# A GRU inside a four-layer kernel: input products in blocks of 24 steps in place of 32

## What is computed

```python
def cell(h, x):
    gi = x @ W_ih + b_ih            # [B, 3 D]: does not depend on h
    gh = h @ W_hh + b_hh            # [B, 3 D]: needs the state before
    i_r, i_z, i_n = jnp.split(gi, 3, axis=-1)
    h_r, h_z, h_n = jnp.split(gh, 3, axis=-1)
    r = jax.nn.sigmoid(i_r + h_r)
    z = jax.nn.sigmoid(i_z + h_z)
    n = jnp.tanh(i_n + r * h_n)
    h_new = (1.0 - z) * n + z * h
    return (h_new, h_new)

_, hs = jax.lax.scan(cell, initial_state, xs)   # 256 steps; B = 8, D = 512
x = x + hs
```

## Time and profile before

| | |
|---|---|
| median of 3 runs | 2070.93 us (2069.5 to 2075.49) |
| the profiled execution | 2068.51 us |
| its span, first to last instruction | 2066.7 us |
| TensorE, busy share of the span | 90% |
| VectorE, ScalarE, GpSimd | 61%, 53%, 18% |
| mean granted clock of TensorE | 0.873 |

### The profile page before, as it was taken

How to read it: one execution, slowest core, us unless ns; L and a number is a source line. 1 busy time by engine, 2 the same in 40 slices (tenths; PEclk the granted TensorE clock), 3 DMA queues, 4 the chain that set the end, 5 groups by cost and what they waited for, 6 DMA issues and landing times. The chain is left out here.

```text
span 2066.7 us, 86137 instructions
## 1 busy us (share of the span) xinstructions
PE 1857.9 (90%) x32542; PEld 1377.3 (67%) x32542; DVE 1257.9 (61%) x5543; ACT 1097.8 (53%) x4105; POOL 377.3 (18%) x1398
## 2 busy tenths in 40 slices
PE   8877998999989989899888899999998999999876
PEld 4234454463644646455556898989898989999875
DVE  5545383654835447363343677777777777777766
ACT  0342736636355363645644565656565655656554
POOL 3000000000000000000000334343434333333335
PEclk7788999999999999999999796969797988879556
DMA  5222213222032220413223000000000000000002
GB/s 175 77 78 53 79 29 94 66 55 87 20 105 56 71 89 1 117 28 73 72 62 108 1 1 0 0 0 0 0 0 0 0 0 0 0 0 0 0 0 82
DMA packets 103527, 86.76 MB, mean 42 GB/s; under 512 B 15616, under 2 KB 90496, under 8 KB 103440
## 3 DMA queue, kind: packets, MB, share of 16 engines
q1 hardware_dynamic: 101392, 84.38, 14.2%
q10 hardware_dynamic: 1664, 1.18, 0.2%
q0 software_dynamic: 384, 0.01, 0.0%
HBM read 60.20 MB, written 21.00 MB: 39 GB/s over the span
## 5 line engine op out<-in xcount | busy, mean ns | idle before, releaser
L1255 PE MATMUL bank_pair_A<-moving,rep 128*128 128x16 f16 x8192 | 327.7, 172 | 55.3 <-DVE moving L1494 49.5
L1255 PEld LDWEIGHTS bank_pair_A<-moving,rep 128*128 128x128 f16 x8192 | 277.8, 99 | 75.6 <-DVE moving L1494 59.1
L1255 PE MATMUL bank_pair_C<-moving,rep 128*128 128x16 f16 x8192 | 321.8, 171 | 0.0
L1255 PE MATMUL bank_pair_B<-moving,rep 128*128 128x16 f16 x8192 | 321.7, 171 | 0.0
L1352 ACT ACTIVATE r_gate<-r_pre 128x16 f32<-128x16 f32 x512 | 110.4, 216 | 301.7 <-DVE r_pre L1443 301.7
L1255 PEld LDWEIGHTS bank_pair_C<-moving,rep 128*128 128x128 f16 x8192 | 266.3, 99 | 0.0
L1255 PEld LDWEIGHTS bank_pair_B<-moving,rep 128*128 128x128 f16 x8192 | 266.3, 99 | 0.0
L1242 PE MATMUL bank_pair_D<-x_part,w_in 128*128 128x256 f16 x1536 | 213.1, 288 | 6.0 <-ACT gi_rz L1379 3.5
L1443 DVE TENSOR_REDUCE r_pre<-bank_pair_A 128x16 f32<-128x32 f32 x512 | 98.1, 192 | 151.5 <-PE bank_pair_A L1255 151.5
L1137 POOL TENSOR_TENSOR x<-x,w_in 128x512 f32<-128x512 f32 x8 | 10.2, 1274 | 964.7 <-DMA w_in<-w_in 964.7
L1043 DVE TENSOR_REDUCE head_max<-bank_pair_A 128x2 f32<-128x1024 f32 x128 | 155.9, 1218 | 38.3 <-PE bank_pair_A L579 38.1
(11 more groups left out here) (260 smaller groups left out, 3632.0 us busy)
## 6 DMA issues: line engine op xcount, KB each, us to landing
rep<-parts SPq DMA_DIRECT2D x256, 64.0 KB
parts<-parts SPq DMA_DIRECT2D x48, 256.0 KB, 2.1
q_rep<-parts SPq DMA_DIRECT2D x32, 256.0 KB, 4.5
k_rep<-parts SPq DMA_DIRECT2D x64, 128.0 KB, 2.8
w_in<-in_x_dram SPq DMA_DIRECT2D x8, 512.0 KB, 4.2
x<-in_x_dram SPq DMA_DIRECT2D x8, 512.0 KB, 4.4
parts<-parts SPq DMA_DIRECT2D x32, 128.0 KB, 2.6
out_dram<-res SPq DMA_DIRECT2D x16, 256.0 KB, 2.1
```

The costliest lines, as they stand in the source:

```text
L1255: last = nc.tensor.matmul(ps[part][:, o:o + 2 * B], w[:, k, (first + c) * P:(first + c) * P + P], moving[j % 2][:, k, :, :].rearrange("p s ...
```

## The change

The blocks of the input products become TS = 24 steps long, 12 chunks at two steps each, so that every step of a block has its half chunk. 256 steps are FULL = 10 blocks of 24 and a last one of 16 (LAST). A matmul of the products has B x 24 = 192 columns in place of 256, in the last block 128. In the loop there are 120 chunks in place of 84 (1920 matmuls in place of 1344).

As the products of block i + 1 now start with the first step of block i, its inputs have to be split earlier: `x_part` has two buffers (`parity`), blocks 0 and 1 are split ahead of the loop by ScalarE and VectorE (8 instructions each of 192 columns in place of 4 of 256), and GpSimd splits block i + 2 during the first 8 steps of block i. The waits of TensorE and ScalarE keep their places. GpSimd waits for an evacuation only in the last chunk of a block (`is_n == 2`) and no more in all four of n. `blocks` calls `run` once per block; two blocks stand in the body of the outer loop, the last two apart, and the loop over chunks is cut in up to four pieces, which makes 16 bodies of two steps. The block sums of the last layer stay sums of 32 steps (`step // TB`). The last 16 steps have gates alone.

The core of the diff:

```diff
+    BODY = 2
+    TS = MC * BODY
+    FULL, LAST = N // TS, N % TS
...
-        x_part = t("x_part", [P, 2, DC, B, TB], F16)
+        x_part = t("x_part", [P, 2, 2, DC, B, TS], F16)
...
-        pG = [pD[:, 0, 0:B * TB], pD[:, 1, 0:B * TB]]
-        BLOCKS = N // TB
-        BODY = 2
-        PLAIN = TB - MC * BODY
...
         def blocks(eng, step, product):
-            with eng.Fori(0, BLOCKS - 1) as blk:
-                with eng.Fori(0, PLAIN // BODY) as k:
-                    for j in range(BODY):
-                        step(blk * TB + k * BODY + j, j, blk, True, k)
-                with eng.Fori(0, RZ) as m:
-                    for j in range(BODY):
-                        step(blk * TB + m * BODY + (PLAIN + j), j, blk)
-                        product(blk + 1, m, j, False)
-                with eng.Fori(RZ, MC) as m:
-                    for j in range(BODY):
-                        step(blk * TB + m * BODY + (PLAIN + j), j, blk)
-                        product(blk + 1, m, j, True)
-            with eng.Fori(0, TB // BODY) as k:
+            def run(first, n, parity, made, split):
+                steps = first * TS
+                ranges = (((0, DC, split), (DC, RZ, None)) if split else ((0, RZ, None),)) + ((RZ, MC - 1, None), (MC - 1, MC, None))
+                for low, high, piece in ranges:
+                    with eng.Fori(low, high) as m:
+                        for j in range(BODY):
+                            step(steps + m * BODY + j, j, piece and (n + 1, 1 - parity, m, piece))
+                            product(n, parity, m, j, (low >= RZ) + (high == MC), made)
+            with eng.Fori(0, (FULL - 2) // 2) as pair:
+                for q in range(2):
+                    run(pair * 2 + q, pair * 2 + (q + 1), 1 - q, TS, TS)
+            run(FULL - 2, FULL - 1, 1, TS, LAST)
+            run(FULL - 1, FULL, 0, LAST, None)
+            with eng.Fori(0, LAST // BODY) as k:
                 for j in range(BODY):
-                    step(k * BODY + (N - TB + j), j, BLOCKS - 1, True)
+                    step(k * BODY + (FULL * TS + j), j)
...
-                        last = nc.tensor.matmul(bank, w_in[w][:, k, bass.ts(m, P)], x_part[:, part, k, :, :].rearrange("p b t -> p (b t)"),
+                        last = nc.tensor.matmul(bank[:, 0:B * width], w_in[w][:, k, bass.ts(m, P)], x_half(parity, part, k, width),
...
-            def product(blk, m, j, is_n):
+            def product(n, parity, m, j, is_n, width):
                 if j == 0:
-                    pe.wait_ge(x_lo, blk * DC + DC)
-                    pe.wait_ge(gi_out, blk * MC + m)
+                    pe.wait_ge(x_lo, n * DC + DC)
+                    pe.wait_ge(gi_out, n * MC + m)
                 for k in range(j * DC // BODY, (j + 1) * DC // BODY):
-                    last = products(m, k, pG[0])
+                    last = products(m, k, pG[0], parity, width)
                 if j == BODY - 1:
...
-            for k in range(DC):
-                nc.scalar.activation(x_part[:, 0, k, :, :], xT[:, k, :, 0:TB], ACT.Copy).then_inc(x_hi, 1)
+            for n in range(2):
+                for k in range(DC):
+                    nc.scalar.activation(x_part[:, n, 0, k, :, :], xT[:, k, :, n * TS:(n + 1) * TS], ACT.Copy).then_inc(x_hi, 1)
...
-                if k is not None:
-                    split(blk + 1, k, j)
+                if split:
+                    split_of(*split, j)
...
-            def product(blk, m, j, is_n):
-                if j == BODY - 2 and is_n:
-
-                    pool.wait_ge(gi_out, blk * MC + m + 1)
+            def product(n, parity, m, j, is_n, width):
+                if j == BODY - 2 and is_n == 2:
+
+                    pool.wait_ge(gi_out, n * MC + m + 1)
```

More of the change, by code:

```diff
@@ L1171, in recurrence @@
         bhh_c = t("bhh_c", [P, MC])
-        later = gi_rz[:, TB:N, :, :].rearrange("p t m b -> p (t m b)")
+        later = gi_rz[:, TS:N, :, :].rearrange("p t m b -> p (t m b)")
         staged = later[:, 0:DC * 3 * D].rearrange("p (c n) -> p c n", c=DC)
@@ L1237, in _, with products, step @@
         def _(pe):
-            def products(m, k, bank):
+            def products(m, k, bank, parity, width):
                 for w in range(2):
                     for part in range(2):
-                        last = nc.tensor.matmul(bank, w_in[w][:, k, bass.ts(m, P)], x_part[:, part, k, :, :].rearrange("p b t -> p (b t)"),
+                        last = nc.tensor.matmul(bank[:, 0:B * width], w_in[w][:, k, bass.ts(m, P)], x_half(parity, part, k, width),
                                                 start=(k == 0 and w == 0 and part == 0), stop=(k == DC - 1 and w == 1 and part == 1))
                 return last
-            def step(step, j, blk, begins=False, k=None):
+            def step(step, j, split=None):
                 pe.wait_ge(seeded, step * 6 + 4)
@@ L1295, in first_products @@
                         pe.wait_ge(x_lo, k + 1)
-                    last = products(m, k, pG[m % 2])
+                    last = products(m, k, pG[m % 2], 0, TS)
                 last.then_inc(gi_ps, 1)
@@ L1405, in _ @@
         def _(dve):
-            for k in range(DC):
-                dve.wait_ge(x_hi, k + 1)
-                nc.vector.tensor_tensor(x_part[:, 1, k, :, :], xT[:, k, :, 0:TB], x_part[:, 0, k, :, :], ALU.subtract).then_inc(x_lo, 1)
+            for n in range(2):
+                for k in range(DC):
+                    dve.wait_ge(x_hi, n * DC + k + 1)
+                    nc.vector.tensor_tensor(x_part[:, n, 1, k, :, :], xT[:, k, :, n * TS:(n + 1) * TS], x_part[:, n, 0, k, :, :],
+                                            ALU.subtract).then_inc(x_lo, 1)
             dve.wait_ge(b_ld, 32)
@@ L1520, in _, with split_of @@
         def _(pool):
-            def split(blk, k, j):
-                src = xT[:, bass.ds(k, 1), :, bass.ts(blk, TB)].rearrange("p o b t -> p (o b) t")
-                hi, lo = (x_part[:, n, bass.ds(k, 1), :, :].rearrange("p o b t -> p (o b) t") for n in range(2))
+            def split_of(n, parity, k, width, j):
+                src = xT[:, bass.ds(k, 1), :, bass.ds(n * TS, width)].rearrange("p o b t -> p (o b) t")
+                hi, lo = (x_part[:, parity, part, :, :, :].rearrange("p c b t -> p c (b t)")[:, bass.ds(k, 1), 0:B * width]
+                          .rearrange("p o (b t) -> p (o b) t", b=B) for part in range(2))
                 if j == 0:
```

25 lines of the change are left out of this document (14 added, 11 removed).

## The result

| | before | after |
|---|---|---|
| median of 4 runs | 2070.22 us | 2171.39 us |
| lowest to highest | 2065.32 to 2075.49 | 2164.62 to 2173.99 |
| mean granted clock of TensorE | 0.873 | 0.737 |

The changed kernel is slower: ratio 1.0483, 95% interval 1.0446 to 1.052, or 101 us by the medians. The prediction said 2168 us. In the text, *before* and *after* are the two kernels, and the experiments go by the labels of the table further down.

A forecast was written before the change was run, and what follows sets the result against it. It took product steps to be bound by TensorE and its clock, and gates-alone steps by waiting for VectorE. Loop +99.4 us and -2.5 before it gave +96.9, hence a median of 2168 us, range 2145 to 2185.

The forecast's parts named there:

- The clock: TensorE in the recurrence loop: granted 1.2 GHz throughout, as 192-column products are too narrow to lift it; chance 0.83.
- the start: Start of the loop: clock already low, since TensorE stands idle for a while before the first step.
- Once low there is nothing in the loop that lifts it: Recurrence loop: the wide products that lifted the clock seven times are gone, so a low clock stays low.
- The step at 1.2 GHz: Loop steps: 3.86 us with 192 columns (gates 2.61, products 1.25), 3.44 with 128, plain steps 3.31.
- The first step: First step of the loop: 5.5 us, from 5.13 and part of one product.
- More loops: Loop bodies, 16 of two steps rather than 4: cost taken as 0, with 3 us for the range.
- The sum for the loop: Whole recurrence loop: 971.0 us against 871.6, +99.4 us.
- Before the loop: First input products and splits ahead of the recurrence, 192 columns wide: -2.5 us.
- Evacuations, splits and the wait for the evacuation: ScalarE and GpSimd work in the loop: no cost behind a TensorE with no idle time.
- The rival at full clock: Loop at 2.4 GHz: products in every step lift the clock, one rise suffices; 2039 us, chance 0.11.

The follow-up runs named there:

- e2: Kernel before with its own loops and waits, but the loop's input-product matmuls stream 192 of 256 columns: 2139.12 us, ratio 1.0331 to before.
- e1: Changed kernel plus two unread 256-column matmuls behind every step's input products (four in the 128-column steps): 2063.97 us, ratio 0.998 to before.
- e4: Changed kernel plus one unread 256-column matmul per step: 2182.46 us, one run.
- e3: Changed kernel plus two unread 256-column matmuls per step in every second block alone: 2098.09 us, ratio 1.0131 to before.
- e9: Changed kernel, outer loop written out, with two unread 256-column matmuls per step in the first block alone: 2147.43 us, ratio 1.0375 to before.
- e5: Changed kernel with its outer loop over pairs of blocks written out, nothing else changed: 2158.75 us, ratio 1.045 to before.
- e6: Changed kernel, outer loop written out and two unread matmuls added per step (four in the 128-column steps): 2043.81 us, ratio 0.9874 to before.
- e7: Kernel before plus seven unread 256-column matmuls behind the gates of every plain step: 2057.47 us, ratio 0.9948 to before.

## Why the prediction was right, point by point

**The clock.** The deciding choice, 1.2 GHz through the loop, was right, and so was its reason: e2 has the narrower products alone and the low clock, e1 has the whole change and, with more work, the full clock. What the prediction claimed on thinner ground was the start. It took for granted that the clock is low there, since TensorE stands idle before the first step. In fact the clock is still up when step 0 begins, in after until 2.7 us into it, and in e4 it did not fall there at all, though TensorE is idle for the same 1.07 us just before that step in both. Why it survived there is not known, so that it did not survive in after was in part luck. The price of that luck has a bound: at each of the five jumps back that were met at 1.00 (three in e1, one each in e3 and e4) the clock fell in the stall, so a start at 1.00 would have lasted two blocks at most in after, some 28 us. In e3 and e9 it was gone in block 1 already.

**"Once low there is nothing in the loop that lifts it."** Shown by e9 (0.50 from the fall in block 1 to the end of the loop, 726.00 us of it in the last line of its windows), by e4 (831 us) and by after itself.

**The step at 1.2 GHz.** 3.86 us was forecast, 3.84 measured: products 1.23 for 1.25, gates 2.61 for 2.61. For 128 columns 3.42 for 3.44, for the plain steps 3.29 for 3.31. Over the loop that is about 5 us too much.

**The first step.** 4.85 us for 5.5: the products filled a wait that was there before.

**More loops.** This is the term that failed. The prediction looked at the body changes of before, found nothing in them, and took 0, with 3 us for the range. What costs is not a change of body but the jump back of the outer loop, whose body had grown from three short loops to eight: 10.9 us in three blocks, and 11.0 us by e5. The price could not be read from before, whose outer loop jumps back without a stall; a rival on the length of the jump was missing.

**The sum for the loop**: +99.4 us forecast, +105.0 measured; about -5 from the size of the step, -0.7 from the first, +10.9 from the jumps. That the program came within 3.4 us of the forecast by the medians (2171.39 for 2168) is thus better than its terms: the missing jumps and the steps that were priced a little too high offset each other in part.

**Before the loop**: -2.5 us forecast, -2.0 measured in this pair; over all traces the stretch takes 29.0 to 31.4 us with the change and 33.4 to 34.5 without, so about -3.5. **Evacuations, splits and the wait for the evacuation** had no price behind a TensorE without gaps, as forecast: in after, steps 23 and 24, around the wait at the change of block, take 4.60 + 3.08 = 7.68 us, which is two ordinary steps of 3.84.

**The rival at full clock.** Its time, 2039 us, was about right for a kernel without the stalls: e6, which has the clock by added work and no jumps back, takes 2043.81; with the jumps, in e1, it is 2063.97. Its mechanism failed: products in every step do not lift the clock, and one rise does not suffice. What it said against the theory, that the clock stays at 1.00 while products run, was read from products of 256 columns and holds for these in every block of before.

## What to carry to other kernels

Work that TensorE does in a latency-bound loop has two effects: its own time, and the clock of everything else on TensorE. Before narrowing, spreading or removing it, look in the windows at the granted clock of each kind of stretch, with and without that work, and cost the change at both levels. If the clock falls because the work got too thin, added matmuls that nobody reads can pay for themselves, as long as they fit into TensorE's idle time at the full clock; and an outer loop whose body has become long may be cheaper written out.

## What was not expected of the hardware

- TensorE can be busy without a single gap in the profile (553.00 of 553.00 us in e5) and be granted 0.50 all the time. The Trainium skill (TensorE: Matmul & The Clock Gate, Part 1: The HAM clock gate) has activity release the throttle; by that rule alone the clock would have risen here; the measurement decides, and being busy without gaps was not enough.
- To hold the clock takes less than to lift it: 192 columns alone held it in two blocks of four (e3), 192 columns and one added matmul for two blocks (e4), and seven added matmuls beside the gates for all later blocks (e7), while none of the three lifted it from 0.50 in any step of these traces. A step is shorter at 1.00 (3.3 us for 3.84), so the same work stands closer together there; the runs do not tell this from a lower need. The case of e4 is a single run.
- The jump back over a long loop body left TensorE idle for 2.8 to 2.9 us in after and for up to 4.1 us in e4, at 0.50, and for 3.9 to 4.7 us where the clock was 1.00 (e1, e3, e4). There the clock falls in the stall and the next steps pay again: 7 to 9 us a jump in e1.
